# Key stacks of 128 rows with zeros, returned in two halves; key norms applied on GpSimd

## The chip, the cores and the metric

One core of one Trainium2 chip. The metric is the device time of one launch in microseconds. Its engines are named as in the profile: PE (TensorE, matmuls), PEld (its weight loads), DVE (VectorE), ACT (ScalarE), POOL (GpSimd), SP (SyncE, which issues all DMAs here; SPq is its queue).

## The reference

```python
# x: (32, 256, 256), context: (32, 77, 256); 8 heads of 128 in the cross-attention, 16 heads of 16 in the second
f_q, f_k, f_v = (proj(q), proj(k), proj(v))            # layer_norm(t) @ w_in.T, split into heads
dots = jnp.einsum('hqnd,hqmd->hqnm', f_q, f_k)
cosine_sim = dots / (qn[..., :, None] * kn[..., None, :])
var_component = jnp.einsum('hqn,hqm->hqnm', q_ratio, k_ratio)
cov_component = cosine_sim * decorr_scale
mixed = cw * cosine_sim + vw * cov_component + ww * var_component
out = jnp.einsum('hqnm,hqmd->hqnd', mixed, f_v)        # then @ w_out.T + b_out
...
x = x + jnp.tanh(g_xattn[0]) * out
...
scores = jnp.einsum('bqd,bkd->bkq', q, k) / 16         # 16 heads of 16, on layernorm(x)
attn = jax.nn.softmax(scores, axis=-1)
z = l2(l2(attended @ Wo) @ Wff); z = gelu(z)
x = x + jnp.tanh(g_ffn[0]) * z
```

`q_ratio`, `k_ratio` come from the variance of a row of `f_q`, `f_k`; `cw`, `vw`, `ww` and `decorr_scale` are eight numbers each, one per head. `f_k` and `f_v` are the same here, since the context serves as both.

## The kernel before

A setup phase (`setup_phase`, some 170 us) splits the weights into pairs of float16 halves `h` and `l`, normalizes the context, and leaves in DRAM `kstat`, whose rows 0 to 7 are one over the norm of each key and rows 8 to 15 its ratio. Then `main_phase` works on 16 pairs of batches, 512 rows of x each. Every engine walks through the same list of steps, `ORDER`, once in a turn; the work of three pairs overlaps in a turn, since `lead` gives each step the pair that it works on (0: the newest, 1: the one before, 2: the one before that). There are 18 turns; the first two and the last two leave steps out. An engine does its instructions strictly in this order, so a step that waits holds up what stands behind it on that engine.

The steps, by name. `fk`: projection of the context rows (PE), stored as `fvp` in halves (`.h` by ACT, `.l` by DVE; this is so for all products that are split). `fk.k`, `kh`, `kl`: the same values times one over the key's norm, `khat` (DVE, L1350), and its halves `kT` (ACT L1195, POOL L1288). `z`, `zT`: normalized rows of x and their transposes. `q`: projection of x, read by DVE for its statistics only (L1362). `G`: `kT` times the weights. `d`: `xT` times `G`, the dots, which DVE scales by `sq` into `mixed` (L1386). `x`: POOL makes `tmp` = key ratio times query ratio (L1296) and adds it to `mixed` (L1301). `V`: `fvp` times `w_out`. `m`: transposes of `mixed`. `y`: their product with `V`, added by DVE to `xb`, which is x plus a bias from POOL (L1277), into `x2S` (L1395). `ln1`, `lpow`, `ln2`, `zz`: the next normalization. `pq`, `pk`, `pv`: projections for the second attention. `S`: a score step, two matmuls (L1154). `M`: the row maximum (DVE, L1428). `X`: exp with its sum (ACT, L1237). `R`: `vsp` = v over the sums (DVE, L1442). `P`: attended values (PE, L1166). `E`, `L`: their halves. `O`: output product, and `F`: norms, gelu and the sum for `out`.

The 16 heads have only 16 channels each. To bring the parts q and k (their halves `h` and `l`) into the right rows, SP stores them to DRAM (step `parts`, L1033: four stores), and loads them back in another arrangement (step `back`, L1042): for c in 0 to 3 and e in 0 to 1, 16 rows of `kstack` and 16 rows of `qstack` with 512 columns for each of 8 heads. A score product contracts over the 64 rows of one half e:

```python
                        last = nc.tensor.matmul(sc[n % SC][:, jj * NQ:(jj + 1) * NQ],
                                                stack["k"][64 * e:64 * e + 64, j, b2 * NQ + k * P:b2 * NQ + (k + 1) * P],
                                                stack["q"][64 * e:64 * e + 64, j, b2 * NQ:(b2 + 1) * NQ],
                                                start=True, stop=True)
```

Scores 0 to 15 of a turn belong to the first batch of the pair (b2 = 0), 16 to 31 to the second. The first one waits until all 16 loads have landed. `krows` holds a piece of `kstat` for the pair, broadcast to all partitions; SP loads it twice in a turn, the norms (`ldk`, L1023) and the ratios (`ldr`, L1027).

Of the kernel before, what the change touches and what calls it, by code (L numbers as in the profile page):

```python
# [813 lines left out]
S17 E0 y0 x3 R3 X16 V5.h V5.l M17 X17 ldk m3 y0.o S18 m3.h m4 M18 m5 P3 m4.h L0 m3.l m5.h X18 S19 m4.l S20 m5.l fk0
M19 M20 S21 z fk0.h y1 E1 X19 L1 X20 fk0.l M21 fk0.k R4 zT0 O0 y1.o zT0.h ln1 X21 S22 fk1 zT0.f O0. M22 S23 lpow O1
fk1.h M23 X22 fk1.l S24 ln2 X23 P4 O1. fk1.k zz0 zT0.l S25 zz0.h zz1 fk2 zz0.l zz1.h kh0 zT1 zz1.l fk2.h S26 kl0 zT1.h
pq0 fk2.l fk2.k zT1.f M24 pq1 pq0.h M25 X24 pq0.l pk0 R5 X25 M26 pq1.h zT1.l S27 pk0.h pk1 pq1.l X26 pk0.l S28 M27
pk1.h P5 X27 pk1.l M28 S29 parts S30 M29 X28 q0 M30 X29 R6 S31 X30 q1 M31 q0.o X31 P6 kh1 R7 back E2 kl1 P7 L2 pv0 E3
# [676 lines left out]
```

## Time and profile before

| | us |
|---|---|
| median of three runs | 1545.8 (1540.1 to 1548.1) |
| the profiled execution | 1551.8 |
| its span, first to last instruction | 1550.1 |
| PE busy | 1377.8 (89%) |
| DVE busy | 1224.7 (79%) |
| ACT busy | 1027.7 (66%) |
| POOL busy | 443.8 (29%) |
| chain that ended last | PE 30%, DVE 26%, issue 13%, ACT 7%, DMA 6% |

Busy time counts an instruction from its start to its end, and these overlap on an engine, by up to 0.2 us for PE, whose ends are modelled. What an instruction costs in a row of others is the distance from its start to the next one's start, its pitch. The chain is the work followed back from the last instruction.

### The profile page before, as it was taken

To read this page: it belongs to the slowest core of one execution; us is meant where nothing else is said; L and a number is where in the kernel's file an instruction comes from. 1 tells how busy PE (TensorE), PEld (TensorE's weight loads), DVE (VectorE), ACT (ScalarE), POOL (GpSimd) and SP (SyncE) were. 2 spreads that over 40 slices of the span, in tenths; PEclk is the share of its full clock that TensorE was granted. 3 is DMA by queue.
4 is the path that set the end of the run, shared out by engine and by line. 5 is a ranking of instruction groups with operands and counts; after the bars stand their busy time and mean duration, and the time that the engine had idled before them with its cause. 6 is when DMAs were issued, how large, how long until landed. Compare 5 with 4: busy or idle time off the path is not lost.

```text
span 1550.1 us, 35088 instructions
## 1 busy us (share of the span) xinstructions
PE 1377.8 (89%) x10624; PEld 817.0 (53%) x10624; DVE 1224.7 (79%) x3180; ACT 1027.7 (66%) x3326; POOL 443.8 (29%) x279
## 2 busy tenths in 40 slices
PE   5888488799999999999999999999999999999855
PEld 2655355455555555555565645555555555555422
DVE  5878656687979888888798888887888889797844
ACT  5564213575767676767677676777776768676766
POOL 1441241314141323233232424141414141414100
PEclk9999599899999999999999999999999999999966
DMA  8420103417070707070716243343535261717060
GB/s 255 142 87 17 31 22 70 72 49 107 16 138 16 138 16 138 16 133 21 111 43 93 61 74 80 60 78 67 86 61 94 51 103 43 111 25 117 15 95 15
DMA packets 125733, 115.12 MB, mean 74 GB/s; under 512 B 8024, under 2 KB 123376, under 8 KB 125680
## 3 DMA queue, kind: packets, MB, share of 16 engines
q1 hardware_dynamic: 125696, 114.66, 38.4%
q8 instruction: 19, 0.31, 0.1%
q14 instruction: 18, 0.15, 0.0%
HBM read 78.40 MB, written 25.32 MB: 67 GB/s over the span
## 4 chain that ended last, share of the span: by engine, by line
PE 30%; DVE 26%; issue 13%; ACT 7%; DMA 6%; SPq 3%; DVEq 1%; POOL 0%; PEldq 0%; ACTq 0%; POOLq 0%; PEld 0%
PE work L749 8%; PE work L751 7%; PE work L750 7%; DVE nm L1428 7%; DMA qstack<-parts 5%; ACT prob L1237 5%; PE score L1154 3%; SPq L1042 3%; PE attended L1166 2%; PE work L1073 2%; DVE vsp L1442 2%; DVE mixed L1386 2%; DVE zz L1408 1%; DVE l2s L1401 1%; DMA parts<-kl 1%
## 5 line engine op out<-in xcount | busy, mean ns | idle before, releaser
L1237 ACT ACTIVATE prob<-score,nm 128x256 f32<-128x256 f32 x1024 | 474.5, 480 | 117.2 <-DVE nm L1428 112.6
L1428 DVE TENSOR_REDUCE nm<-score 128x2 f32<-128x512 f32 x512 | 336.1, 682 | 32.0 <-PE score L1154 31.2
L1154 PE MATMUL score<-qstack,kstack 64*128 64x256 f16 x1024 | 184.2, 281 | 42.1 <-DMA qstack<-parts 22.9
L1237 ACT ACTIVATION_READ_ACCUMULATOR prob<-score,nm 128x1 f32 x1024 | 216.4, 211 | 0.0
L1362 DVE BATCH_NORM_STATS2 qst<-work 128x6 f32<-128x128 f32 x512 | 111.1, 284 | 72.0 <-PE work L751 70.8
L1166 PE MATMUL attended<-prob,vsp 128*32 128x256 f32 x2048 | 143.4, 399 | 22.4 <-DVE vsp L1442 22.4
L1154 PEld LDWEIGHTS score<-qstack,kstack 64*128 64x128 f16 x1024 | 59.2, 96 | 175.3 <-ACT prob L1237 90.7
L1301 POOL TENSOR_TENSOR mixed<-mixed,tmp 128x616 f32<-128x616 f32 x64 | 96.0, 1501 | 177.4 <-DVE mixed L1386 173.7
L1281 POOL TENSOR_TENSOR rq<-qft,mhalf 128x32 f32<-128x32 f32 x16 | 87.0, 5439 | 144.8 <-DVEq L1369 144.8
L1288 POOL TENSOR_TENSOR kTl<-khat,kTh 128x462 f16<-128x462 f32 (+1 forms) x48 | 46.3, 966 | 253.8 <-ACT kTh L1195 253.8
L749 PE MATMUL work<-woutTh,fvph 128*128 128x256 f16 x384 | 107.3, 279 | 0.0
L750 PE MATMUL work<-woutTl,fvph 128*128 128x256 f16 x384 | 106.6, 278 | 0.0
L751 PE MATMUL work<-woutTh,fvpl 128*128 128x256 f16 x384 | 106.5, 277 | 0.0
L749 PE MATMUL work<-wTh,xTh 128*128 128x512 f16 x256 | 98.3, 384 | 4.3 <-DVE xTl L1356 2.4
L1166 PEld LDWEIGHTS attended<-prob,vsp 128*32 128x32 f32 x2048 | 54.9, 112 | 83.0 <-issue 47.0
L1216 ACT ACTIVATE Gh<-work 128x462 f16<-128x462 f32 (+1 forms) x96 | 47.5, 512 | 76.8 <-PE work L751 75.9
L750 PE MATMUL work<-wTl,xTh 128*128 128x512 f16 x256 | 97.8, 382 | 0.0
L751 PE MATMUL work<-wTh,xTl 128*128 128x512 f16 x256 | 97.8, 382 | 0.0
L1442 DVE TENSOR_TENSOR vsp<-v,rs 128x128 f32<-128x128 f32 x128 | 79.7, 622 | 16.9 <-DVE rs L1436 4.3
L749 PE MATMUL work<-Vph,mTh 128*128 128x256 f16 (+1 forms) x320 | 89.3, 279 | 0.0
L750 PE MATMUL work<-Vpl,mTh 128*128 128x256 f16 (+1 forms) x320 | 88.6, 277 | 0.0
L751 PE MATMUL work<-Vph,mTl 128*128 128x256 f16 (+1 forms) x320 | 88.6, 277 | 0.0
(291 smaller groups left out, 3573.7 us busy)
## 6 DMA issues: line engine op xcount, KB each, us to landing
krows<-kstat SPq DMA_DIRECT2D x32, 616.0 KB, 5.8
kstack<-parts SPq DMA_DIRECT2D x128, 128.0 KB, 7.8
qstack<-parts SPq DMA_DIRECT2D x128, 128.0 KB, 8.3
s_xin<-in_x SPq DMA_DIRECT2D x8, 1024.0 KB, 6.0
xin<-in_x SPq DMA_DIRECT2D x16, 512.0 KB, 7.4
x<-x2S SPq DMA_DIRECT2D x16, 512.0 KB, 5.3
out<-zb SPq DMA_DIRECT2D x16, 512.0 KB, 4.9
parts<-qh SPq DMA_DIRECT2D x16, 256.0 KB, 2.2
```

The lines of the kernel that those rows point to most:

```text
L749: nc.tensor.matmul(out, a["h"][at], b["h"][bt], start=first, stop=False)
L750: nc.tensor.matmul(out, a["h"][at], b["l"][bt], start=False, stop=False)
L751: return nc.tensor.matmul(out, a["l"][at], b["h"][bt], start=False, stop=last)
L1154: last = nc.tensor.matmul(sc[n % SC][:, jj * NQ:(jj + 1) * NQ], stack["k"][64 * e:64 * e + 64, j, b2 * NQ + k * P:b2 * NQ + (k + 1) * P], ...
L1166: last = nc.tensor.matmul(pvb[t][32 * j:32 * j + 32, 0:NQ], vsp[:, e, k, j, :], prob[:, n % PG, k, j, :], start=(e == 0 and k == 0), stop= ...
L1216: nc.scalar.activation(dst, src, ACT.Copy, scale=scale).then_inc(hi_ready[lead(e)], 1)
L1237: nc.scalar.activation(prob[:, g % PG, k, u % 4, :], sc[n % SC][:, jj * NQ:(jj + 1) * NQ], ACT.Exp, bias=nm[:, u:u + 1], accum_out=sums[:, ...
L1281: nc.gpsimd.tensor_tensor(rq[:], qft[:, 0, :, :], w["mhalf"][:].rearrange("p (t h) -> p t h", h=H), ALU.pow).then_inc(rq_ready, 1)
L1301: nc.gpsimd.tensor_tensor(mixed[:, t % 2, :], mixed[:, t % 2, :], tmp[:], ALU.add).then_inc(mixed_ready, 1)
L1362: last = nc.vector.bn_stats(qst[:, t, 4 * half + h, :], bank(e)[:, h * DH:(h + 1) * DH])
L1428: nc.vector.tensor_reduce(nm[:, 2 * n:2 * n + 2], sc[n % SC][:, :].rearrange("p (u q) -> p u q", q=NQ), AX.X, ALU.max, negate=True).then_i ...
L1442: nc.vector.tensor_tensor(vsp[:, e, :, :, FD * e:FD * (e + 1)], src, bc(rs[:, units].rearrange("p (k j) -> p k j", k=KT).unsqueeze(3), [P, ...
```

## The change

It does five things. The key stack gets a second plane: for e = 0 its rows 64 to 127 are zeros, for e = 1 its rows 0 to 63; POOL writes the zeros once, and a score product contracts over all 128 rows of `qstack`. The return of the stacks is cut into `back0` and `back1`, one for each batch, with 16 loads of half the columns each, and the scores wait for their own half. `khat`, `kT` and their steps are gone: G works on `fvp`, and POOL multiplies the scaled dots by one over the key's norm, a third instruction in each x step; both parts of `krows` are loaded at once. `xb` is gone: x is loaded a second time (`ldy`), into `x2S`, where POOL adds the bias. And `ORDER` is another list.

```diff
-xb G0 G0.h G1 G2 G1.h G0.l G2.h G1.l G3 ldr G2.l G4 qs1 G3.h ldx V0 G4.h S0 V0.h G3.l S1 qpow S2 G4.l G5 M0 V1 G5.h
...
+qs1 S0 G0 S1 G0.h G1 S2 G1.h G2 G0.l qpow G2.h G1.l G3 G2.l G4 ldr M0 G3.h V0 M1 G4.h X0 G3.l G4.l G5 V0.h M2 S3 V1
...
-    krows = sb("krows", [P, H, PM])
-    fvp, kT, G, Vp = pair("fvp", [P, PADW]), pair("kT", [P, H, PM]), pair("G", [P, KT, H * PM]), pair("Vp", [P, 2, HT, DIM])
+    krows = sb("krows", [P, 2, H, PM])
+    fvp, G, Vp = pair("fvp", [P, PADW]), pair("G", [P, KT, H * PM]), pair("Vp", [P, 2, HT, DIM])
...
-    stack = {a: sb(a + "stack", [P, FH // 2, PR], F16) for a in "qk"}
+    qstack, kstack = sb("qstack", [P, FH // 2, PR], F16), sb("kstack", [P, 2, FH // 2, PR], F16)
...
+                elif step == "ldy":
+
+                    sp_wait(zz_ready, a)
+                    sp_wait(x2_in, a * 16)
+                    sp.dma_start(x2S[:], x_rows[bass.ds(a * PR, PR), :].rearrange("(t p) d -> p t d", p=P)).then_inc(y_in, 16)
                 elif step == "ldr":
 
                     sp_wait(mixed_ready, a * PT)
+                    sp.dma_start(krows[:], kstat[:, bass.ds(a * PM, PM)].rearrange("(s h) n -> s h n", h=H)
+                                 .partition_broadcast(P)).then_inc(kr_in, 16)
...
-                elif step == "back":
-
-                    sp_wait(parts_stored, a * 64 + 64)
-                    sp_wait(sc_ready, a * SCORES + START)
+                elif step in ("back0", "back1"):
+
+                    b2 = int(step[-1])
+                    cols = slice(b2 * NQ, (b2 + 1) * NQ)
+                    if b2 == 0:
+                        sp_wait(parts_stored, a * 64 + 64)
+                    sp_wait(sc_ready, a * SCORES - (1 - b2) * SCORES // 2 + SC_CREDIT)
                     for c in range(4):
                         for e in range(2):
...
+                            rows = slice(64 * e + FD * c, 64 * e + FD * (c + 1))
+                            for dst, n in ((kstack[rows, e, :, cols], 2 + c // 2), (qstack[rows, :, cols], c % 2)):
+                                src = parts[n].rearrange("(q e d) n -> e d q n", e=2, d=FD)[e][:, :, cols]
+                                sp.dma_start(dst, src).then_inc(stack_in[b2], 16)
...
-                                        w["wN"], (ALL, h, slice(k * P, (k + 1) * P)), kT, (ALL, h))
+                        keys = {half: key_cols(half, h, h + 1) for half in "hl"}
+                        last = products(nc, bk[:, (h - lo_h) * PM:(h - lo_h + 1) * PM].rearrange("p (b m) -> p b m", m=MK),
+                                        w["wN"], (ALL, h, slice(k * P, (k + 1) * P)), keys, (ALL,))
...
-                    if n == 0:
-                        pe.wait_ge(stack_in, b * 256 + 256 + START)
+                    if n % (SCORES // 2) == 0:
+                        pe.wait_ge(stack_in[b2], b * 256 + 256 + START)
...
-                                                stack["k"][64 * e:64 * e + 64, j, b2 * NQ + k * P:b2 * NQ + (k + 1) * P],
-                                                stack["q"][64 * e:64 * e + 64, j, b2 * NQ:(b2 + 1) * NQ],
+                                                kstack[:, e, j, b2 * NQ + k * P:b2 * NQ + (k + 1) * P],
+                                                qstack[:, j, b2 * NQ:(b2 + 1) * NQ],
...
+            nc.gpsimd.memset(kstack[:], 0.0).then_inc(init, 1)
...
                 if e == "xb":
 
-                    pool.wait_ge(x_ready, a * 16 + 16)
-                    pool.wait_ge(v2_ready, a)
-                    nc.gpsimd.tensor_tensor(xb[:], xin[:], bc(w["tb"][:].unsqueeze(1), [P, PT, DIM]),
+                    pool.wait_ge(y_in, a * 16 + 16)
+                    nc.gpsimd.tensor_tensor(x2S[:], x2S[:], bc(w["tb"][:].unsqueeze(1), [P, PT, DIM]),
                                             ALU.add).then_inc(xb_ready, 1)
...
                     pool.wait_ge(tmp_ready, a * PT + t + 1)
                     wait_drained(pool, a, f"d{2 * t}", f"d{2 * t + 1}")
+                    rows = mixed[:, t % 2, :].rearrange("p (h m) -> p h m", m=MK)
+                    nc.gpsimd.tensor_tensor(rows, rows, krows[:, 0, :, (t // 2) * MK:(t // 2 + 1) * MK],
+                                            ALU.mult).then_inc(dotted, 1)
+                    pool.wait_ge(dotted, a * PT + t + 1)
                     nc.gpsimd.tensor_tensor(mixed[:, t % 2, :], mixed[:, t % 2, :], tmp[:], ALU.add).then_inc(mixed_ready, 1)
...
-                elif part == "k":
-
-                    lo_h, hi_h = HEAD_PARTS[int(c)]
-                    dve.wait_ge(rk_in, a * 16 + 16)
-                    ins = nc.vector.scalar_tensor_tensor(
-                        khat[:, lo_h:hi_h, :], bank(e)[:, 0:(hi_h - lo_h) * PM].rearrange("p (h n) -> p h n", n=PM), KS,
-                        krows[:, lo_h:hi_h, :], ALU.mult, ALU.mult)
                     drain(ins, e)
```

What the order moves, at the three places of which the prediction speaks. First SP's queue from the last store of `parts` to the store of the result, in the loop over turns; `kstack` and `qstack` are the loads of `back`. Before:

```order
L1033 DMA parts<-kl 128x2x512
L1005 ISA
L1005 ISA [waits parts_stored]
L1042 DMA kstack<-parts 16x8x512 [waits sc_ready]
L1042 DMA qstack<-parts 16x8x512
...
L1053 ISA [waits ob_ready]
L1053 DMA out<-zb 128x4x256
```

With the change:

```order
L1035 DMA parts<-kl 128x2x512
L1005 ISA
L1005 ISA [waits parts_stored]
L1048 DMA kstack<-parts 16x8x256 [waits sc_ready]
L1048 DMA qstack<-parts 16x8x256
...
L1005 REGISTER_ALU
L1048 DMA kstack<-parts 16x8x256 [waits sc_ready]
L1048 DMA qstack<-parts 16x8x256
...
L1058 ISA [waits ob_ready]
L1058 DMA out<-zb 128x4x256
```

The loads are of 256 columns instead of 512, and a second row of eight pairs stands behind the first, ahead of the store of the result; only its first load waits, for the scores of the turn.

Second, PE at the turn of the loop, up to the first score (`wTh,xTl` is the end of q7, `wNh` is G, `woutTh` the end of V0). Before:

```order
L751 MATMUL work<-wTh,xTl 128x512
L988 UNCONDITIONAL_BRANCH
L988 ISA
L1090 ISA [waits drained0]
L749 MATMUL work<-kTh,wNh 128x154 [waits kT_ready]
L750 MATMUL work<-kTl,wNh 128x154
...
L751 MATMUL work<-woutTh,fvpl 128x256
L1149 ISA
L1151 ISA [waits stack_in]
L1154 MATMUL score<-qstack,kstack 128x256 [waits exp_done]
L1154 MATMUL score<-qstack,kstack 128x256
```

With the change (`wvh,zzTl` is the end of pv1):

```order
L751 MATMUL work<-wvh,zzTl 128x256
L987 UNCONDITIONAL_BRANCH
L987 ISA
L1158 ISA [waits stack_first]
L1161 MATMUL score<-qstack,kstack 128x256 [waits exp_done]
L1161 MATMUL score<-qstack,kstack 128x256
L937 ISA
L934 ISA [waits drained0]
L749 MATMUL work<-fvph,wNh 128x154 [waits drained0]
L750 MATMUL work<-fvpl,wNh 128x154
```

The first score stands ahead of G0, right behind pv1; before, G0 to G4 and V0 stood ahead of it, and pv1 in the middle of the q steps.

Third, POOL's x steps, x0 and the beginning of x1. Before:

```order
L1295 REGISTER_ALU [waits wqr_ready,kr_in]
L1296 TENSOR_TENSOR tmp<-krows,wqr 128x616 [waits mixed_ready]
L1299 REGISTER_ALU
L934 ISA [waits tmp_ready]
L1301 TENSOR_TENSOR mixed<-mixed,tmp 128x616 [waits drained1,drained0]
L1296 TENSOR_TENSOR tmp<-krows,wqr 128x616 [waits mixed_ready,wqr_ready,kr_in]
```

With the change:

```order
L1290 REGISTER_ALU [waits wqr_ready,kr_in]
L1291 TENSOR_TENSOR tmp<-krows,wqr 128x616 [waits mixed_ready]
L1294 REGISTER_ALU
L934 ISA [waits tmp_ready]
L934 ISA [waits drained2]
L1297 TENSOR_TENSOR mixed<-mixed,krows 128x616 [waits drained0]
L1300 TENSOR_TENSOR mixed<-mixed,tmp 128x616 [waits dotted]
L1291 TENSOR_TENSOR tmp<-krows,wqr 128x616 [waits mixed_ready,wqr_ready,kr_in]
```

A multiplication by `krows`, the key norms, stands between the two that were there, and behind the wait for the dots.

## Rows read from the trace of the kernel before

**Rows 1.** Windows: one turn; us, busy of PE, PEld, DVE, ACT, POOL, PEclk, DMA share, GB/s

```profile
748.73:829.47 80.74, 75.92 (x626) 44.79 (x625) 69.02 (x169) 58.40 (x196) 24.13 (x15) 1.00 0.43 74
```

**Rows 2.** Timeline, SP's queue: first store of parts, 13 turns apart; start, duration

```profile
425.67 0.37 SPq L1033 DMA_DIRECT2D parts<-qh  x1
...
1470.06 0.36 SPq L1033 DMA_DIRECT2D parts<-qh  x1
```

**Rows 3.** Waits of PE in that turn, first and last of seven (4.5 us)

```profile
PE attended L1166 <- DVE vsp L1442: 1.4, 2, 1.1
...
PE work L749 <- DVE qst L1362: 0.2, 1, 0.2
```

**Rows 4.** Waits of DVE in that turn, first and last of ten (9.6 us)

```profile
DVE qst L1362 <- PE work L751: 4.0, 2, 3.6
...
DVE qft L786 <- DVE qft L770: 0.2, 1, 0.2
```

**Rows 5.** Timeline, SP's queue, one turn

```profile
747.99 0.37 SPq L1033 DMA_DIRECT2D parts<-qh  x1
...
752.67 0.33 SPq L1042 DMA_DIRECT2D kstack<-parts  x1
...
759.67 0.43 SPq L1042 DMA_DIRECT2D qstack<-parts  x1
...
771.43 0.41 SPq L1027 DMA_DIRECT2D krows<-kstat  x1
...
828.73 0.37 SPq L1033 DMA_DIRECT2D parts<-qh  x1
```

**Rows 6.** Timeline, PE: the turn's first score products

```profile
773.42 0.82 PE L1154 MATMUL score<-qstack,kstack 64*128 64x256 f16 x6 [0.81 <-DMA qstack<-parts]
```

**Rows 7.** Timeline, PE: a score pair between projections, one before a P step

```profile
824.60 0.38 PE L750 MATMUL work<-zzTl,wkh 128*128 128x512 f16 x1
824.81 0.38 PE L751 MATMUL work<-zzTh,wkl 128*128 128x512 f16 x1
825.12 0.39 PE L1154 MATMUL score<-qstack,kstack 64*128 64x256 f16 x2
825.45 0.39 PE L749 MATMUL work<-zzTh,wkh 128*128 128x512 f16 x1
...
826.85 0.39 PE L1154 MATMUL score<-qstack,kstack 64*128 64x256 f16 x2
827.17 1.07 PE L1166 MATMUL attended<-prob,vsp 128*32 128x256 f32 x16
```

**Rows 8.** Windows (columns as Rows 1): the stacks' return; a load of key rows

```profile
756.00:770.00 14.00, 13.23 (x88) 7.26 (x86) 10.22 (x34) 8.53 (x20) 4.67 (x3) 1.00 1.17 111
...
802.00:806.00 4.00, 4.00 (x44) 2.55 (x42) 3.20 (x6) 3.09 (x10) 0.00 (x0) 1.00 0.80 154
```

**Rows 9.** Groups by line and form: busy, mean ns; idle before

```profile
L1442 DVE TENSOR_TENSOR vsp<-v,rs 128x128 f32<-128x128 f32 x128 | 79.7, 622 | 16.9 <-DVE rs L1436 4.3
L1350 DVE SCALAR_TENSOR_TENSOR khat<-work,krows 128x462 f32<-128x462 f32 x32 | 20.2, 631 | 0.3 <-DMA krows<-kstat 0.3
L1301 POOL TENSOR_TENSOR mixed<-mixed,tmp 128x616 f32<-128x616 f32 x64 | 96.0, 1501 | 177.4 <-DVE mixed L1386 173.7 <-POOL tmp L1296 3.4
```

**Rows 10.** Timeline, POOL and DVE: the extra step and what it holds up

```profile
778.52 1.23 POOL L1296 TENSOR_TENSOR tmp<-krows,wqr 128x616 f32<-128x616 f32 x1 [1.03 <-DMA krows<-kstat]
786.33 1.22 POOL L1296 TENSOR_TENSOR tmp<-krows,wqr 128x616 f32<-128x616 f32 x1 [0.17 <-POOL mixed L1301]
...
786.58 1.12 DVE L1442 TENSOR_TENSOR vsp<-v,rs 128x128 f32<-128x128 f32 x1
```

**Rows 11.** One line's instructions, L1442: ns min/median/max

```profile
L1442 DVE TENSOR_TENSOR vsp<-v,rs x128: 291/293/1470, 296.3 to 1531.8; 128x128 f32<-128x128 f32 x128
```

**Rows 12.** Timeline, PE: first turn with m0; first scores of the last turn

```profile
224.04 1.07 PE L1117 MATMUL work<-ident,mixed 128*128 128x128 f32 x8 [0.83 <-POOL mixed L1301]
...
1494.02 1.46 PE L1154 MATMUL score<-qstack,kstack 64*128 64x256 f16 x6 [8.78 <-DMA qstack<-parts]
```

More of the change, by code:

```diff
@@ L814 @@
[L814 to L818, printed above, removed]
@@ L819 @@
-kh2 L3 q1.o O2 pv0.v O3 O2. q2 O3. q3 F1 q2.o pv1 q3.o kl2 F2 q4 pv1.v q5 q4.o F3 q6 q5.o q7 q6.o q7.o F4 out res
+qs1 S0 G0 S1 G0.h G1 S2 G1.h G2 G0.l qpow G2.h G1.l G3 G2.l G4 ldr M0 G3.h V0 M1 G4.h X0 G3.l G4.l G5 V0.h M2 S3 V1
+G5.h V0.l X1 G5.l X2 qs2 S4 M3 d0 V1.h M4 S5 X3 V1.l d1 ldy ldx d0.o X4 d2 d1.o M5 S6 S7 M6 d3 X5 x0 R0 V2 X6 M7 S8 P0
+d2.o X7 M8 d3.o S9 V2.h S10 X8 M9 V3 M10 X9 R1 x1 S11 V3.h V4 M11 X10 V2.l S12 V4.h P1 M12 X11 V3.l S13 X12 V4.l xb m0
+M13 m1 m0.h R2 S14 d4 m1.h m0.l X13 S15 m1.l m2 m2.h d4.o d5 E0 M14 S16 d5.o P2 X14 m2.l x2 M15 d6 M16 X15 S17 L0 V5
@@ L820 @@
+q5 q3.o F3 q4.o q6 back1 q5.o q7 q6.o pv0 q7.o F4 pv1 pv0.v pv1.v out res
 """.split()
@@ L829, in lead @@
         return 2
-    return 0 if step.split(".")[0].rstrip("0123456789") in ("z", "zT", "fk", "kh", "kl", "q", "ldx", "ldk") else 1
+    return 0 if step.split(".")[0].rstrip("0123456789") in ("z", "zT", "fk", "q", "ldx") else 1
 HALVES = [[s[:-2] for s in ORDER if s.endswith(".h") and s[:2] != "zT" and lead(s) == n] for n in range(2)]
@@ L952, in emptied @@
             lo_h, hi_h = HEAD_PARTS[c]
-            rows = fvp[half][:, 0:2 * H * PAD].rearrange("p (n c) -> p n c", c=PAD)
-            return (rows[:, 2 * lo_h:2 * hi_h, 127:PAD],
+            return (key_cols(half, lo_h, hi_h),
                     bk[:, 0:(hi_h - lo_h) * PM].rearrange("p (n m) -> p n m", m=MK), FV / WS)
@@ L996, in _ @@
         def _(sp):
-            for waited in (stack_in, ob_ready, vs_ready, sc_ready, stored):
+            for waited in (*stack_in, ob_ready, vs_ready, stored):
                 sp.sem_inc(waited, START)
+            sp.sem_inc(sc_ready, SC_CREDIT)
             sp.sem_inc(exp_done, EXP_CREDIT)
@@ L1038, in a_part @@
                     for c in range(4):
                         for e in range(2):
-                            for name, n in (("k", 2 + c // 2), ("q", c % 2)):
-                                src = parts[n].rearrange("(q e d) n -> e d q n", e=2, d=FD)[e]
-                                sp.dma_start(stack[name][64 * e + FD * c:64 * e + FD * (c + 1), :, :],
-                                             src).then_inc(stack_in, 16)
+                            rows = slice(64 * e + FD * c, 64 * e + FD * (c + 1))
@@ L1190, in a_part @@
                 e, _, part = e.partition(".")
-                if e in ("kh0", "kh1", "kh2"):
-                    lo_h, hi_h = HEAD_PARTS[int(e[-1])]
-                    wait_drained(act, a, "fk" + e[-1])
-                    nc.scalar.activation(kT["h"][:, lo_h:hi_h, :], khat[:, lo_h:hi_h, :], ACT.Copy).then_inc(kT_half, 1)
-                elif e[:-1] == "zT" and part in ("h", "f"):
+                if e[:-1] == "zT" and part in ("h", "f"):
                     c, bk = int(e[-1]), bank(e)
```

64 lines of the change are left out of this document (26 added, 38 removed).

## The prediction

> **What bounds the kernel now.** I read the windows of one turn first, then the waits of PE and of DVE, then SP's queue. The program is a setup, two turns without scores, and 16 turns with 32 score steps each. I call T0 the moment at which SP issues the first store of `parts`; it comes once in a turn, 16 times in all, so 15 full intervals lie between them. The reader is to see that an interval takes 80.7 us in the middle [rows 5], 80.3 us on average over 13 of them [rows 2], and that in one of them PE is busy 75.9 us and DVE 69.0, at the full clock, 2.4 GHz [rows 1]. PE waits for others 4.5 us in it [rows 3], so it is occupied for 80.7 - 4.5 = 76.2 us. DVE waits 9.6 us [rows 4], so it is occupied for 71.1. **PE's queue is the bound and DVE stands close behind it**; ACT (58.4 busy) and POOL (24.1) are not. DVE's longest wait, 4.0 us, is for the projections of q, the stage in which PE has work and DVE little.
>
> That stage exists because of a round trip. After T0 the four stores take until the first load of the stacks is issued at T0 + 4.7, the last of 16 loads is issued at T0 + 11.7 [rows 5], and PE's first score of the turn runs at 773.42, T0 + 25.4, after waiting 0.8 us for the last load [rows 6]. Until then PE fills the time with q, O, pv, G and V.
>
> **The change, part by part.**
>
> *128-row scores.* A matmul of 512 columns starts 0.21 to 0.22 us after the one before. From the last projection to the score pair it is 0.31, and from the pair, which needs 2 x 0.11, to the next projection 0.33 [rows 7]. A score step between ordinary products thus costs about 0.42 us where its columns ask for 0.22: 0.10 is lost on going in and 0.10 on coming out. The likeliest reason is that the array is regrouped, since these are the only products on 64 rows. In the timeline of that turn I count 17 runs of score steps with ordinary products on both sides and 8 next to a P step, which is itself in another shape, so that only one side is saved there. This gives 17 x 0.2 + 8 x 0.1 = **4.2 us a turn** off PE. The bounds are 0 (the gap stays) and 32 x 0.2 = 6.4. The Trainium skill, "TensorEngine Tiling (Array Packing)", section Theoretical Speedup, speaks against the padding: a contraction of 64 rows may run as two tiles side by side, up to 2 times as fast. In the trace the pair is not side by side (0.22 plus the two losses), since both of its products use the same half of the rows; by the rule a kernel that paired the halves would stand 32 x 0.11 = 3.5 us a turn better than this one, which neither of the two kernels does.
>
> *Return in two halves.* The loads are bound by bytes at 111 GB/s while they run [rows 8]. 2 MB at that rate is 18.9 us; the observed T0 + 4.7 to T0 + 25.3 is 1.7 more. The first half has 16 loads of 64 KB, 1 MB: 4.7 + 9.4 + 1.7 = T0 + 15.9. Below it is bounded by issue, 0.47 us from one load to the next [rows 5], 16 x 0.47 = 7.5 us, so T0 + 13.9. Above, if a packet costs the same at 512 bytes as at 1 KB, a half costs what the whole did: T0 + 25.3. I take the byte rate, as packets of 616 bytes move at 154 GB/s [rows 8], faster than is needed here. In the new order PE has after T0: P7 1.1 [rows 7]; q1 to q7, O2 and O3, six products of 512 columns each, 9 x 1.3 = 11.7; pv0 and pv1, 24 of 256 columns, 2.6; or 15.4 us. So **the wait for the stacks stays near 0.5 us**, and G, V0 and V1 run beside scores instead of ahead of them. The second half lands where the whole did, T0 + 25.3, half a turn before score 16.
>
> *Key norms.* khat (two of 0.63 and one shorter) goes from DVE, about 1.5 us a turn at its pitch [rows 9], and three activations from ACT and three subtractions from POOL, which nothing waits for long. POOL gets four multiplications of 616 columns, priced as the addition of that size, 1.50 us each [rows 9]: 6.0 us a turn. Each stands in the chain d, x, m. x0 starts with a product of 1.23 us when the key rows land, 778.52, T0 + 30.5 [rows 10]. One load of 1232 KB instead of 616 adds 616 KB at 154 GB/s, 4.0 us: T0 + 34.5. x0 and x1 then take 2 x (1.23 + 1.50 + 1.50) = 8.5, so m0 may start at T0 + 43. PE gets to m0 after 14 scores, at (76.6 - 16) / 32 = 1.9 us a score from T0 + 16: T0 + 42.6. The cost is 0.4 us; 0 to 3 is possible.
>
> *What POOL does to DVE.* vsp needs 0.29 us alone and 0.62 on average [rows 9, 11]; at 786.58 it takes 1.12 and ends with the product that POOL began at 786.33 [rows 10]. That is 8 x 0.33 = 2.6 us a turn for 10.9 us of x steps, 0.24 us per us. The new multiplications add 6.0 x 0.24 = **1.5 us on DVE**, 0 to 6.0. DVE's occupation stays at 71.1 - 1.5 + 1.5 = 71.1 us.
>
> *Rest.* The second load of x (512 KB) and the third use of x2S as xb lie in queues that are empty then: 0. POOL's memset of the key stack stands before the first turn, where POOL has nothing to do until qpow: 0 to 1 us, once.
>
> *Sum of a turn.* PE 76.2 - 4.2 = 72.0 occupied; its waits 4.5, less 0.3 for the stacks and plus 0.4 for m0: **76.6 us, 4.1 less**. DVE's 71.1 leaves 5.5 for its waits, of which the q stage keeps 4.0: it just fits. Bounds: 73.5 if most waits go, 79.2 if DVE keeps 8 us of its 9.6.
>
> *The ends.* In the first turn with x steps nothing else covers them, and PE waited 0.8 us for m0 already [rows 12]; four multiplications are 6.0, some of it behind V: +4. After the last T0 (1470.06 [rows 2]) the first score ran at 1494.02 [rows 12], 24.0 later, with nothing to fill the time; now 15.9, so -8.0, and about -1.3 for scores at the low clock.
>
> *Total.* 15 x -4.1 = -61.5, +4, -9.3: -66.8. The profiled execution took 1551.8 us for a span of 1550.1; it becomes 1485.0. It lies 6.0 above the median of the three runs, 1545.8, so I forecast **1479 us**.
>
> **The rivals.**
>
> *A. The halves are bound by packets, not bytes (slower).* Then the first half lands at T0 + 25.3, PE has 15.4 us of work before it and stands idle 9.4 more: a turn of 86, 15 x 5.3 + 4 = +83, **1629 us**. It decides from a loss of 4.1 us a turn on, that is when one 64 KB load takes over (15.4 + 4.1 - 4.7 - 1.7) / 16 = 0.82 us instead of 0.59. For it: the new pieces are smaller than any that this path has shown. Against: 616-byte pieces at 154 GB/s.
>
> *B. DVE becomes the bound.* Scores crowd it, POOL holds its vsp and DVE keeps 8 us of waits: 79.2 a turn, 15 x -1.5 + 4 - 9.3, **1518 us**. The Trainium skill, "SBUF — State Buffer", section Who interferes with whom, says that a vector instruction with two SBUF inputs and a GpSimd one that reads SBUF exclude each other for a whole instruction, and the trace agrees (vsp, 1.12 against 0.29). If each of the four multiplications held DVE for its whole 1.50 us where PE waits, a turn would be 4.5 longer than in my sum, 81.1, and the total about **1546 us**, no change.
>
> *C. The padding saves nothing.* If the gap of 0.10 comes with semaphores and not with the shape, a turn stays at 80.8 and only the end gains: **1541 us**. Against: V, y and q steps also begin with a wait for a semaphore and follow at their pitch.
>
> *D. The waits melt with the gaps*, as they are DVE's lateness in the score stage, which now starts 9.5 us earlier: 73.5 a turn, **1432 us**.
>
> **How the numbers follow.** Forecast 0.57, A 0.09, B as 1518 0.16 and as no change 0.03, C 0.07, D 0.08. A measurement here tells 0.5%, about 8 us, from no change. Faster: 0.57 + 0.16 + 0.08 = 0.81. C and the second form of B come to 0.10, of which 0.02 could land above the edge: same 0.08, slower 0.09 + 0.02 = 0.11. The range takes in D nearly and B: 1436 to 1518.
>
> **What would show it.** The profile of the changed kernel should show an interval between first stores of `parts` of 76 to 77 us; from the last projection to a score pair 0.22 us and from the pair on 0.22; the first score of a turn 16 us after T0; additions and multiplications of 1.5 us on POOL, and vsp at a mean of 0.65 to 0.85 us. I am wrong if the interval is above 79 us, if DVE's waits stay at 9 us, or if the first score stands later than T0 + 18.

## The result, and the profile after

The changed kernel takes **1594.5 us** (median of four runs, 1592.4 to 1596.5), the kernel before 1546.7 us on the same chip: a ratio of 1.031, 95% interval 1.029 to 1.034. It is slower by 3.1%; the forecast was 1479 us. The page of its profiled execution (share of the span by engine; the granted clock in 40 slices; the chain that ended last):

```profile
span 1594.7 us, 35158 instructions
...
PE 1344.9 (84%) x10624; PEld 882.7 (55%) x10624; DVE 1181.2 (74%) x3132; ACT 997.1 (63%) x3278; POOL 493.3 (31%) x296
...
PEclk9999699998999999899999899989999999999977
...
PE 21%; SPq 15%; ACT 13%; DMA 13%; issue 10%; POOL 9%; DVE 7%; POOLq 0%; DVEq 0%; ACTq 0%; PEldq 0%; PEld 0%
```

PE is busy less than before, in a longer span. The chain no longer runs mostly over PE and DVE but over SP's queue, the DMAs, ACT and POOL; in its list by line, the loads of the stacks on SP's queue hold 12% and the load of `krows` 10%. The sum over the program: the first T0 moved from 257.7 to 267.4 (+9.7), the 15 intervals from 80.8 to 83.6 us on average (+41.6), and the piece from the last T0 to the end from 80.0 to 73.3 (-6.7). That is the 44.6 us between the two spans.

One of the shorter turns, T0 at 772.17, with a stretch of it, in windows (columns as in Rows 1), which answers to [rows 1]:

```profile
772.17:854.51 82.34, 73.59 (x626) 48.82 (x625) 65.01 (x166) 56.58 (x191) 26.84 (x16) 0.98 0.42 79
812.17:816.17 4.00, 2.20 (x11) 2.02 (x12) 0.42 (x1) 0.79 (x2) 3.92 (x3) 0.64 0.00 0
```

Its waits of PE, the two longest of six (8.8 us in all, 4.5 before [rows 3]):

```profile
PE work L1124 <- POOL mixed L1300: 5.7, 1, 5.7
PE work L1124 <- DVE x2S L1383: 1.0, 1, 1.0
```

SP's queue in that turn, which answers to [rows 5] (`krows` is issued behind all 32 loads of the stacks):

```profile
772.17 0.37 SPq L1035 DMA_DIRECT2D parts<-qh  x1
...
776.85 0.32 SPq L1048 DMA_DIRECT2D kstack<-parts  x1
...
791.44 0.43 SPq L1048 DMA_DIRECT2D qstack<-parts  x1
792.35 0.41 SPq L1058 DMA_DIRECT2D out<-zb  x1
793.15 0.50 SPq L1053 DMA_DIRECT2D x<-x2S  x1
794.38 0.41 SPq L1027 DMA_DIRECT2D krows<-kstat  x1
...
854.51 0.37 SPq L1035 DMA_DIRECT2D parts<-qh  x1
```

POOL's x0 and x1 in the same turn, timeline:

```profile
805.01 1.22 POOL L1291 TENSOR_TENSOR tmp<-krows,wqr 128x616 f32<-128x616 f32 x1 [10.43 <-DMA krows<-kstat]
806.48 1.38 POOL L1297 TENSOR_TENSOR mixed<-mixed,krows 128x616 f32<-128x616 f32 x1 [0.25 <-POOL tmp L1291]
807.94 1.49 POOL L1300 TENSOR_TENSOR mixed<-mixed,tmp 128x616 f32<-128x616 f32 x1
809.60 1.22 POOL L1291 TENSOR_TENSOR tmp<-krows,wqr 128x616 f32<-128x616 f32 x1 [0.17 <-POOL mixed L1300]
810.98 1.38 POOL L1297 TENSOR_TENSOR mixed<-mixed,krows 128x616 f32<-128x616 f32 x1 [0.16 <-POOL tmp L1291]
812.44 1.48 POOL L1300 TENSOR_TENSOR mixed<-mixed,tmp 128x616 f32<-128x616 f32 x1
```

And PE around m0, timeline, with the first score of the turn ahead of it:

```profile
788.49 0.39 PE L1161 MATMUL score<-qstack,kstack 128*128 128x256 f16 x2 [0.42 <-DMA qstack<-parts]
...
807.86 0.39 PE L1161 MATMUL score<-qstack,kstack 128*128 128x256 f16 x2
813.97 1.97 PE L1124 MATMUL work<-ident,mixed 128*128 128x128 f32 x8 [5.72 <-POOL mixed L1300]
815.73 0.63 PE L1161 MATMUL score<-qstack,kstack 128*128 128x256 f16 x2
```

Read these three together. `krows` is issued at T0 + 22.2, behind 32 loads of stacks and two stores, and lands 11.0 us later (median; 5.8 for half the size before). POOL begins x0 at T0 + 32.8 and ends x1 at T0 + 41.8. PE had come to m0 at T0 + 36.1 and stood there for 5.7 us. Around the end of that idle stretch the granted clock was 0.64 on average over 4 us, a mixture of 1.2 and 2.4 GHz. It fell while PE still stood, the eight transposes of m0 took 1.97 us, and it was back at 2.4 GHz by 816.8. About 2.8 us of work at half speed are 1.4 us lost. The wait and the low clock make 7.1 us; without them this turn would be 75.2.

Most turns lose more than this one. PE comes to m0 at T0 + 36.1 in 13 of the 15 intervals, waits for it 94.1 us in 16 waits over the whole run, and the granted clock is 0.92 to 0.98 in the 15 intervals, against 1.00 in 11 of 15 before. The longest one, in windows:

```profile
433.88:519.98 86.10, 76.44 (x626) 50.98 (x625) 64.71 (x166) 56.80 (x191) 26.76 (x16) 0.92 0.41 76
```

The score products did gain what they were meant to. Around a pair in PE's timeline:

```profile
820.48 0.29 PE L751 MATMUL work<-Gh,xTl 128*128 128x308 f16 x1
820.62 0.38 PE L1161 MATMUL score<-qstack,kstack 128*128 128x256 f16 x2
820.83 0.27 PE L749 MATMUL work<-woutTh,fvph 128*128 128x256 f16 x1
```

The pair starts 0.14 after the product of 308 columns before it, which is that product's own pitch, and the next product starts 0.21 after the pair, which is the pair's 2 x 0.11. The two losses of 0.10 [rows 7] are gone. The first score runs at T0 + 16.3.

### The profile page after: what moved, and what is told of

It is laid out like the page before. It is cut to its first block, busy times and chain, and to the rows that moved or that the text cites. A ratio compares the mean times of both kernels' runs of the same rounds, so it can differ in the third digit from the quotient of the medians.

```text
span 1594.7 us, 35158 instructions
## 1 busy us (share of the span) xinstructions
PE 1344.9 (84%) x10624; PEld 882.7 (55%) x10624; DVE 1181.2 (74%) x3132; ACT 997.1 (63%) x3278; POOL 493.3 (31%) x296
## 4 chain that ended last, share of the span: by engine, by line
PE 21%; SPq 15%; ACT 13%; DMA 13%; issue 10%; POOL 9%; DVE 7%; POOLq 0%; DVEq 0%; ACTq 0%; PEldq 0%; PEld 0%
SPq L1048 12%; DMA krows<-kstat 10%; ACT prob L1239 8%; PE work L749 5%; PE work L750 5%; PE work L751 5%; POOL mixed L1300 3%; POOL mixed L1297 3%; DMA parts<-kl 3%; POOL tmp L1291 2%; DVE z L1332 2%; PE work L1124 2%; PE score L1161 2%; PE attended L1173 1%; ACT junk L1256 1%
## 5 line engine op out<-in xcount | busy, mean ns | idle before, releaser
L1416 DVE TENSOR_REDUCE nm<-score 128x2 f32<-128x512 f32 x512 | 341.0, 684 | 41.3 <-PE score L1161 38.9
L1239 ACT ACTIVATION_READ_ACCUMULATOR prob<-score,nm 128x1 f32 x1024 | 228.5, 223 | 0.0
L1161 PE MATMUL score<-qstack,kstack 128*128 128x256 f16 x1024 | 194.7, 285 | 30.4 <-DMA qstack<-parts 18.0
L1124 PE MATMUL work<-ident,mixed 128*128 128x128 f32 (+1 forms) x320 | 63.0, 345 | 115.9 <-POOL mixed L1300 94.1
L1161 PEld LDWEIGHTS score<-qstack,kstack 128*128 128x128 f16 x1024 | 89.3, 101 | 100.6 <-ACT prob L1239 36.0
L1308 POOL TENSOR_TENSOR nrs<-nrm,phalf 128x8 f32<-128x8 f32 x16 | 26.2, 1636 | 354.5 <-ACT zb L1258 354.5
L1291 POOL TENSOR_TENSOR tmp<-krows,wqr 128x616 f32<-128x616 f32 x64 | 78.8, 1231 | 174.2 <-DMA krows<-kstat 168.8
L1218 ACT ACTIVATE mTh<-work 128x512 f16<-128x512 f32 (+1 forms) x96 | 47.1, 534 | 126.8 <-PE work L1124 126.7
L1340 DVE SCALAR_TENSOR_TENSOR mTl<-work,mTh 128x512 f16<-128x512 f32 (+1 forms) x96 | 54.7, 598 | 94.9 <-ACT mTh L1218 94.8
L1124 PEld LDWEIGHTS work<-ident,mixed 128*128 128x128 f32 (+1 forms) x320 | 46.7, 175 | 128.6 <-POOL mixed L1300 90.5
L1297 POOL TENSOR_TENSOR mixed<-mixed,krows 128x616 f32<-128x616 f32 x64 | 89.4, 1396 | 58.7 <-DVE mixed L1375 49.3
```

The lines of the kernel that those rows point to most:

```text
L1124: last = nc.tensor.transpose(bk[0:HM_ROWS[t], (2 * n + r) * P:(2 * n + r + 1) * P], mixed[:, r, t * P:t * P + HM_ROWS[t]], ident[:])
L1239: nc.scalar.activation(prob[:, g % PG, k, u % 4, :], sc[n % SC][:, jj * NQ:(jj + 1) * NQ], ACT.Exp, bias=nm[:, u:u + 1], accum_out=sums[:, ...
L1291: nc.gpsimd.tensor_tensor(tmp[:].rearrange("p (h m) -> p h m", m=MK), krows[:, 1, :, (t // 2) * MK:(t // 2 + 1) * MK], bc(wqr[:, t, :].uns ...
L1297: nc.gpsimd.tensor_tensor(rows, rows, krows[:, 0, :, (t // 2) * MK:(t // 2 + 1) * MK], ALU.mult).then_inc(dotted, 1)
L1416: nc.vector.tensor_reduce(nm[:, 2 * n:2 * n + 2], sc[n % SC][:, :].rearrange("p (u q) -> p u q", q=NQ), AX.X, ALU.max, negate=True).then_i ...
```

## The experiments

All times are medians; ratios are to the kernel before on the same chip. An edit is to the changed kernel unless it says otherwise. Theory 1: the key rows come late because of where their load stands in SP's queue, and PE stands at m0 for them. Theory 2: the multiplications on GpSimd cost the time, wherever the rows are. Experiments 1 to 4, 5 to 8 and 9 to 12 are three sessions, in which the kernel before took 1542.1, 1543.0 and 1547.3 us (1546.7 beside the changed kernel), so a difference of medians across sessions is good to about 5 us.

**1. The key rows loaded early.**

```diff
-... G2.l G4 ldr M0 ...
+... G2.l G4 M0 ...
-... M18 x3 z S20 ...
+... M18 x3 ldr z S20 ...
-("z", "zT", "fk", "q", "ldx")
+("z", "zT", "fk", "q", "ldx", "ldr")
```

> The changed kernel, with the load of the key rows (ldr) moved on SP's queue from behind the two returns of the stacks to right behind x3 of the turn before, some 27 us ahead of T0; it loads for the next pair there. Theory 1 (late key rows): in the changed kernel krows is issued at T0 + 22.2 and its x steps begin at T0 + 32.8, so x1 ends at T0 + 41.8 while PE stands at m0 from T0 + 36.1; that costs 5.9 us of wait and about 1.5 us of half clock behind it in each turn. With the rows there early, x0 can start at T0 + 24 (query norms) and x1 ends by T0 + 35, so the wait for m0 falls below 1 us, the granted clock stays at 1.00 there, a turn takes 76 to 77.5 us instead of 83.6, and the total is 1485 to 1505 us. Theory 2 (the four multiplications on GpSimd are the cost, through the longer chain and DVE's locks, whenever the rows land): the gain is at most 1 us a turn, total 1580 or more.

Measured: 1507.3 us, 0.977 (0.974 to 0.979), 87 us less than the changed kernel and less than the kernel before; 2 us above the range of Theory 1. POOL, timeline of a turn with T0 = 654.22:

```profile
676.60 1.22 POOL L1291 TENSOR_TENSOR tmp<-krows,wqr 128x616 f32<-128x616 f32 x1
681.28 1.39 POOL L1297 TENSOR_TENSOR mixed<-mixed,krows 128x616 f32<-128x616 f32 x1 [3.46 <-DVE mixed L1375]
...
687.89 1.52 POOL L1300 TENSOR_TENSOR mixed<-mixed,tmp 128x616 f32<-128x616 f32 x1
```

x1 now ends at T0 + 35.2. In two neighbouring turns, windows:

```profile
577.10:654.22 77.12, 72.52 (x626) 47.82 (x625) 65.26 (x165) 56.58 (x191) 26.81 (x16) 1.00 0.46 84
654.22:732.99 78.77, 74.16 (x626) 48.90 (x625) 65.25 (x165) 56.53 (x191) 26.82 (x16) 0.98 0.46 83
```

There is no wait for m0 in either. They differ by 1.65 us of low clock only, which Theory 1 had not expected here. Seven of the 15 intervals have such a stretch, at about T0 + 55. Theory 1 explains the larger part of the loss, 87 of the 115 us between the forecast and the changed kernel; Theory 2 as it was stated is out.

**2. No multiplication by the norms** (this part of the computation is left out), rows still late.

```diff
-                    nc.gpsimd.tensor_tensor(rows, rows, krows[:, 0, :, (t // 2) * MK:(t // 2 + 1) * MK],
-                                            ALU.mult).then_inc(dotted, 1)
-                    pool.wait_ge(dotted, a * PT + t + 1)
```

> The changed kernel without the multiplication by one over the key's norm on GpSimd (this part of the computation is left out); krows is loaded as before, late. Theory 1: x0 and x1 end 2 x 1.46 us earlier, so of the 5.9 us that PE waits for m0 3 remain, and part of the low clock; a turn takes 79.5 to 80.5, total 1530 to 1550 us. Theory 2: all of the loss goes with the multiplications, the wait for m0 falls below 1 us and the total to 1500 or less.

Measured: 1511.5 us, 0.980 (0.978 to 0.983). In PE's waits of one turn (T0 = 730.09) the one for m0 is what was expected:

```profile
PE work L1124 <- POOL mixed L1296: 3.1, 1, 3.1
```

3.1 us instead of 5.7, a turn of 78.5. But the total is 83 us lower, not 50: some 8.6 us in the first turn (its T0 is 258.8, not 267.4), and in each turn something besides m0. Neither theory had that, and the total lies 18 us below the range of Theory 1. DVE's timeline has one thing that changed (experiment 6 says more): a group of four `z` instructions takes 1.38 us in this run and 3.69 in the changed kernel.

**3. Scores on 64 rows.** `kstack[64 * e:64 * e + 64, e, ...]` and `qstack[64 * e:64 * e + 64, ...]` in the product, nothing else.

> The changed kernel with score products on 64 rows of the same stacks (the padding unused). Theory 1: the 13 scores ahead of m0 lie in time that PE would wait anyway, so only the other 19 cost: 19/32 of 4.2 us, 2.5 us a turn, total about 1630 us; the gaps around a score pair are back at 0.10 on each side. If PE's occupation set the whole turn, it would be 4.2 us a turn, 1658 us. If the padding had saved nothing (rival C of the prediction), 1594 us.

Measured: 1631.0 us, 1.055 (1.050 to 1.060). The padding is worth 36 us even here, and Theory 1's number holds. The trace agrees with its reason: PE comes to m0 later, at T0 + 37.3 to 37.8 in 13 of 15 intervals, and waits for it less, by 24.7 us over these intervals, so what the scores ahead of m0 cost is mostly taken from the wait. The comparison is not quite clean: with 64 rows the four `z` instructions take 2.62 us instead of 3.69, as they meet only one of POOL's instructions.

**4. The kernel before, scores over 128 rows.** `stack["k"][:, j, ...]` and `stack["q"][:, j, ...]`, nothing else; each score then sums both halves of the channels.

> The kernel before with score products over all 128 rows of both stacks (no zero planes: the sums mix the two halves of the channels, so the scores are others; shape and work of every other instruction are the same). It measures the padding in the old order by itself. By the prediction's sum: 4.2 us a turn off PE, 15 x 4.2 plus 1.3 at the end, total about 1482 us, if DVE lets it through; if DVE is the bound close behind (rival B) about 1.5 us a turn, 1525 us; if nothing is saved 1546 us. I expect 1490 to 1505, since DVE kept 9.6 us of waits.

Measured: 1532.1 us, 0.993 (0.990 to 0.996), a gain of 10 us, far from the 1490 to 1505 expected and 7 us short of the 1525 of rival B. One turn in windows, and PE's two longest waits in it:

```profile
736.59:815.82 79.23, 73.08 (x625) 47.82 (x626) 67.50 (x169) 58.71 (x194) 24.12 (x15) 1.00 0.43 75
```

```profile
PE attended L1166 <- DVE vsp L1442: 1.7, 2, 1.1
PE score L1154 <- ACT prob L1237: 1.7, 5, 0.4
```

PE's waits in the turn sum to 6.2 us, so it is occupied for 73.0 us, 3.2 less than before the change of shape; the turn is only 1.5 shorter than [rows 1], because PE's waits grew from 4.5 to 6.2 us, over the whole run those for ACT's `prob` from 14.1 to 25.7. The chain that ended last now goes over DVE for 30% of the span and over PE for 26% (26% and 30% before). In the old order the score stage, DVE's maxima and ACT's exp with it, takes back half of what PE saves.

**5. The early rows with scores on 64 rows** (edits 1 and 3 together).

> The kernel with the early key rows (1507 us) and score products on 64 rows of the same stacks. With no wait for m0 left, PE's occupation sets the turn, so the padding should be worth its full 4.2 us a turn here: 77.9 + 4.2 = 82.1, total 1507 + 15 x 4.2 + 1.3, about 1570 us, slower than the kernel before. If DVE shares the bound (rival B) it is worth half of that or less: 1540 or below.

Measured: 1554.6 us, 1.007 (1.005 to 1.010), between the two expectations. The padding is worth 47 us in this order, against 10 in the old one and 36 with the late rows; here too `z` is held less with 64 rows (2.62 us instead of 3.80), so 47 is rather too little. How much the padding gives depends on the order. What the new order gives by itself was not tried: no run has it with the key norms where they were.

**6. The early rows without the multiplications** (edits 1 and 2; that part of the computation is left out).

> The kernel with the early key rows and no multiplication by the key norms on GpSimd (left out of the computation). It measures what the multiplications cost when the rows are there in time. Prediction's terms: 4 us in the first turn and up to 1.5 us a turn through DVE's locks where DVE counts. If PE alone sets the turn: only the first turn's 5 to 8 us, total about 1500 us. If the locks count: 15 x 1.5 more, 1478 us.

Measured: 1450.6 us, 0.941 (0.939 to 0.943): 57 us for the multiplications where the rows are not late, 3.3 us a turn and 6 in the first (of the 3.3, about 0.8 is the low clock of seven turns, which has gone too). That is beyond the upper of the two expectations, 29 us. Where it goes stands in DVE's timeline of experiment 1; the first line is the first of four `z` instructions, the second the group of four:

```profile
700.73 1.59 DVE L1332 TENSOR_SCALAR z<-xin,st 128x256 f32<-128x256 f32 x1
```

```profile
700.73 3.80 DVE L1332 TENSOR_SCALAR z<-xin,st 128x256 f32<-128x256 f32 x4
```

and POOL at the same time:

```profile
700.78 1.39 POOL L1297 TENSOR_TENSOR mixed<-mixed,krows 128x616 f32<-128x616 f32 x1 [0.23 <-POOL tmp L1291]
702.25 1.49 POOL L1300 TENSOR_TENSOR mixed<-mixed,tmp 128x616 f32<-128x616 f32 x1
```

The first z ends just behind POOL's multiplication and the second just behind its addition; only then do the last two follow at their own pace. POOL's two instructions are no longer than elsewhere, though the first z is recorded 0.05 us ahead of the multiplication. Four z take 3.80 us. In the kernel before, with POOL idle, DVE's timeline has:

```profile
807.80 1.38 DVE L1333 TENSOR_SCALAR z<-xin,st 128x256 f32<-128x256 f32 x4
```

The changed kernel has the same picture, z first, POOL second (here the first z slips through and the second and third are held):

```profile
824.03 3.69 DVE L1332 TENSOR_SCALAR z<-xin,st 128x256 f32<-128x256 f32 x4
```

```profile
824.20 1.48 POOL L1297 TENSOR_TENSOR mixed<-mixed,krows 128x616 f32<-128x616 f32 x1 [0.23 <-POOL tmp L1291]
825.76 1.49 POOL L1300 TENSOR_TENSOR mixed<-mixed,tmp 128x616 f32<-128x616 f32 x1
```

The Trainium skill, "SBUF — State Buffer", section Who interferes with whom, names `tensor_scalar` among the DVE operations that can take both ports and then exclude GpSimd for a whole instruction. The trace agrees: 1.59 us for one z beside a multiplication of 1.39, against 0.41 alone (the mean in the kernel before). The longest case stands in the first turn: POOL's memset of the zeros, 7.06 us, held one z for 7.09 us. Little came of it: the first T0 of experiment 2, which has this memset, is 1.1 us later than in the kernel before.

```profile
177.03 7.06 POOL L1273 MEMSET kstack<- 128x8192 f16 x1
```

```profile
176.66 8.22 DVE L1332 TENSOR_SCALAR z<-xin,st 128x256 f32<-128x256 f32 x4
```

**7. The kernel before, return in two halves, nothing else.**

> The kernel before with the return in two halves and nothing else, in its own order. In it G0 to G4 and V0 stand ahead of the first score, which waits only 0.8 us for the stacks, so a turn can gain at most 0.8 us; the last turn, where nothing fills the time, gains up to 8 us. Expected 1527 to 1540 us. If the halves were bound by packets (rival A), there would be no gain at the end, and 1546 us or more.

Measured: 1533.8 us, 0.993 (0.991 to 0.996), as expected. Thirteen of the 15 intervals stay at 79.9 to 80.8 us; the gain is in the ends. The stretch behind the last T0 is 73.4 us instead of 80.0. Between the profiled executions the first two intervals are shorter too (77.9 and 80.6 against 83.0 and 84.9), with less low clock in them. The first scores of its last turn (T0 = 1458.69), PE's timeline:

```profile
1475.78 0.92 PE L1161 MATMUL score<-qstack,kstack 64*128 64x256 f16 x6 [3.38 <-DMA qstack<-parts]
```

T0 + 17.1 instead of 24.0. So the half does not take the time of the whole, as it would if packets bound it.

**8. The early rows, and z elsewhere.** z goes to a place where POOL is idle (edit 1 and this one):

```diff
-... M18 x3 ldr z S20 ...
+... M18 x3 ldr S20 ...
-... m5.l M22 S24 ...
+... m5.l M22 z S24 ...
```

> The kernel with the early key rows and one step moved in the order: z (four DVE instructions of 0.95 us in a row, 3.8 us) from behind x3 to behind M22. In the 1507 us kernel PE waits behind that block for Vpl (0.4) and x2S (1.0), ACT waits 3.6 us for a maximum, and in about half of the turns PE's clock falls to half for 3.4 us right after (78.8 against 77.1 us a turn). Theory (the block starves PE, and the low clock follows from it): the waits and the low spells go, a turn takes 75.5 to 76.5 us, total 1475 to 1490 us. Rival (PE's occupation is the bound and the low clock has another cause): no change or within 5 us of 1507.

Measured: **1464.9 us, 0.951 (0.948 to 0.953)**, the fastest of the kernels that leave nothing out, 42 us below experiment 1 and 10 below the range of the theory. z in DVE's timeline, and one turn in windows:

```profile
694.96 1.38 DVE L1332 TENSOR_SCALAR z<-xin,st 128x256 f32<-128x256 f32 x4
```

```profile
641.20:716.12 74.92, 72.02 (x626) 47.91 (x625) 62.68 (x165) 56.50 (x191) 27.20 (x16) 1.00 0.48 87
```

z takes 1.38 us again, no low clock is left in that turn, and 14 of 15 intervals are 74.9 to 76.1 us. PE waits 3.0 us, so it is occupied for 71.9.

**9. The same without the multiplications** (left out of the computation).

> The 1465 us kernel (early key rows, z behind M22) without the multiplications by the key norms (left out of the computation). With z beside x3 they cost 57 us (1507 to 1451). Theory: most of that was one collision, the four z instructions taking 3.8 us beside POOL's multiplication and addition of x3 instead of 1.4, and the starved stretch behind them; now z stands where POOL is idle, so leaving them out gives only the first turn's 5 to 6 us and the one vsp that is held (0.9 us a turn): total 1444 to 1456 us. Rival: the multiplications cost 3.4 us a turn wherever z stands: total 1410 us.

Measured: 1440.3 us, 0.931 (0.928 to 0.934). 24.6 us are left of the 57 (20.9 between the spans of the profiled executions: 4.2 in the first turn and 1.1 in each interval). So the larger part, 32 us by the medians and 36 by the spans, went with the collision with z, the low clock behind it included. The rest is a little more than expected: 1440 us is 4 below the range.

**10. z elsewhere with the rows still late.**

> The changed kernel with z moved behind M22 and nothing else: krows is still loaded late. If the two costs are separate (wait for m0; z held by POOL), it gains what z gave with the early rows, 42 us: 1550 us. If the late rows are the one bound of the loop, since ldr waits for x3, nothing is gained, 1590 us. I expect 1545 to 1565: PE's path from m0 to the next T0 gets shorter and the path from T0 to m0 stays.

Measured: 1566.9 us, 1.014 (1.010 to 1.017), 28 us less than the changed kernel, between "separate" (42) and "nothing" and 2 above the range. The wait for m0 in one turn:

```profile
PE work L1124 <- POOL mixed L1300: 6.5, 1, 6.5
```

The wait is what it was, 97.3 us over the run against 94.1, so nothing is given back in front of m0. Where the other 14 us are shows in the intervals. Moving z gave 2.2 us a turn in the turns of experiment 1 that have no low clock (77.1 to 74.9), and gives 2.0 here on average (83.6 to 81.6). With the early rows it also took away the low clock of seven turns, 1.65 us each. Here the low clock comes with the wait for m0 and stays, a granted clock of 0.94 to 0.98 in every interval. The two costs are nearly separate.

**11. The second half of the stacks behind the key rows**: `back1` stands behind `ldr`, in the next turn of the loop, and `ldr` keeps its place in its turn.

```diff
-... q6 back1 q5.o ...
+... q6 q5.o ...
-... G2.l G4 ldr M0 ...
+... G2.l G4 ldr back1 M0 ...
```

> The changed kernel with the second half of the return (back1) moved on SP's queue behind the store of the result and the load of krows, in the next turn of the loop; ldr keeps its place in its turn. krows is then issued 7.7 us earlier, at about T0 + 14.5, and starts behind 1 MB of stacks instead of 2. Theory 1 (place in SP's queue and what is ahead of it in the transfers): x1 ends by T0 + 36, the wait for m0 is 0 to 1 us, total 1500 to 1515 us, as with the early load; the second half lands near T0 + 32, well ahead of score 16. If it is the size of the load (1232 KB at once) that matters, the rows stay late: over 1560 us.

Measured: 1506.4 us, 0.973 (0.970 to 0.977), the same as experiment 1 and within Theory 1's range. SP's queue in one turn:

```profile
738.09 0.37 SPq L1035 DMA_DIRECT2D parts<-qh  x1
...
755.63 0.41 SPq L1027 DMA_DIRECT2D krows<-kstat  x1
```

The load is issued at T0 + 17.5, behind one half only, POOL begins x0 at T0 + 27.9 and PE waits 0.5 us for m0. It is as large as before, so the size alone does not make it late; moving it up in the queue is enough. (The size is in the time to landing all the same: 616 KB took 5.8 us before, 1232 KB 7.8 with the stacks long landed.) (It is issued 4.7 us earlier, not the 7.7 expected: SP waits 3.2 us for DVE's `zb`, which the store of the result ahead of it needs.)

**12. V3 ahead of P0** in the kernel of experiment 8 (`M7 S8 V3 P0`).

> The 1465 us kernel with V3 moved ahead of P0, so that PE has 1.6 us of work while POOL's addition of x0 holds vsp (1.54 us instead of 0.29), where it now waits 0.9 us. If the wait is simply covered: 15 x 0.9 off, 1452 us. If another wait takes its place (V3's bank, the scores behind): within 4 us of 1465.

Measured: 1499.8 us, 0.970 (0.966 to 0.973), 35 us slower than experiment 8 (39 between the spans of the profiled executions); both expectations missed. PE's longest wait in a turn:

```profile
PE work L749 <- DVE mixed L1375: 1.8, 1, 1.8
```

V3 needs a bank that DVE empties with a `mixed` step, and that step stands behind the very `vsp` that POOL holds. PE now waits for it ahead of P0 and of the score behind, and DVE then waits 2.2 us for that score. A second `vsp` is held as well, the one behind that score, 1.72 us instead of 0.29. PE comes to m0 at T0 + 38.9 instead of 37.1.

## Why the prediction was wrong

By its own steps, in its order:

- *128-row scores*: right in the mechanism. The losses on both sides of a pair are gone. PE's occupation fell by 3.2 us in the old order (experiment 4) and to 71.9 in the new (experiment 8), against 4.2 and 72.0 predicted. Whether it reaches the total depends on the order: 10, 36 or 47 us.
- *Return in two halves*: right. The first score stood at T0 + 16.3, predicted near 16, and the wait for the stacks was 0.4 us. Rival A is out, by this and by experiment 7.
- *Key norms*, **"PE gets to m0 after 14 scores, at 1.9 us a score from T0 + 16: T0 + 42.6. The cost is 0.4 us; 0 to 3 is possible."** This step failed. Its half about POOL was right: rows at T0 + 32.8 (34.5 predicted), x1 done at T0 + 41.8 (43). PE came to m0 at T0 + 36.1, 6.5 us earlier than I had it. I had spread the 32 scores evenly over the turn, but the projections stand in the other part of it; in the stretch up to m0 PE has 13 scores, not 14, and needs 19.8 us for all that stands there, 1.5 us a score. The order had shown what stands there. The cost, for which the sum had 0.4, was 5.7 us in the turn shown and 94.1 us in 16 waits over the run, and on top the low clock around the end of the wait, of which the prediction had nothing: 1.4 us in the turn shown, more in most others. Taking this away gave 87 us (experiment 1), with experiment 11 as the second way.
- *What POOL does to DVE*: **"The new multiplications add 6.0 x 0.24 = 1.5 us on DVE"**. This step failed too. The hold is real, but I priced it from `vsp`, by a mean over the turn, and let DVE's spare time take it, so that the turn paid nothing. In the new order `vsp` is held less (mean 367 ns, 622 before [rows 9]); what is held is `z`, which I did not look at: its mean went from 412 to 1077 ns (1008 without the four of the first turn). That is 2.3 us in one block, and PE and ACT wait behind it. With the early rows DVE is busy 65.25 us in a turn with the multiplications (experiment 1, T0 at 890.45) and 62.54 without (experiment 6, T0 at 856.97). These 2.7 lie within my 0 to 6.0; but the turn pays 3.3, where my sum had nothing. Moving z gave 42 us, or 28 with the late rows.
- *Rest*: the second load of x shows no cost in the turn read here, where POOL does not wait for it; no run tests it. The memset of the zeros cost about the 1 us that I had allowed, though it held DVE for 7 us.
- *The ends*: the first T0 came 9.7 us later, predicted 4; leaving out the multiplications alone takes 8.6 of it back, so the term was mis-sized and is almost wholly theirs. The tail gained 6.7, predicted 9.3: in the last turn the first load of the stacks is issued at T0 + 6.1 (4.6 in the kernel before) and the first scores ran at T0 + 18.1, not 15.9:

```profile
1539.48 1.46 PE L1161 MATMUL score<-qstack,kstack 128*128 128x256 f16 x6 [6.21 <-DMA qstack<-parts]
```

Rival B had a part in both failures of size: a faster PE meets DVE's and ACT's stage in the old order (experiment 4), and POOL holds DVE, but on another instruction than I had named. Rival C is out, and D's "waits melt" came true only in part: 3.0 us of waits in experiment 8, a turn of 74.9, between D's 73.5 and my 76.6. With the two failed steps repaired, by two moves in the order, the kernel takes 1465 us where I had said 1479. None of the rivals was the case that came: late key rows. I had the numbers for it, T0 + 43 against T0 + 42.6, and gave a meeting of two chains within 0.4 us a cost of 0 to 3, when an error of 6.5 in either arrival costs 6.5.

What stays open: why the granted clock falls in some turns of experiment 1 without a wait over 1 us in them (654.22 to 732.99) and not in others with nearly the same waits; in experiment 8 it falls in the first interval only. In the last turn SP waits 4.0 us for the last store of `parts`, 2.5 in the kernel before; why that store takes longer is open too. And what the 1.1 us a turn of experiment 9 consist of was not tried; `vsp`, at a mean of 438 ns with the multiplications and 294 without, 8 times a turn, would be 1.2 us, all of it, if each hold reached PE.

## What to carry to other kernels

- Where two chains meet, compute both arrivals from the work that stands in front of each, step by step, in the new order; the mean pace of a turn is no arrival time. Give the meeting the error of the arrivals as its range.
- On a queue that works in order, look at what is ahead of the load, not only at what it waits for: here two moves, the load a turn earlier or half of the stacks behind it, gave 87 and 88 us for the same bytes.
- Before more work goes to GpSimd, list what DVE does beside it in the new order, `tensor_scalar` included, and keep blocks of such instructions away from it.

## What the hardware showed that I had not expected

- A `tensor_scalar` of 128x256 with one tensor input in SBUF was held for a whole GpSimd instruction, 1.59 us instead of 0.41, and the next one for the following instruction again.
- The same happened beside a GpSimd memset, which reads no tensor: 7.06 us of memset, one `z` of 7.09 us.
- An idle stretch of 5.7 us on PE had a price behind it: the next 2.8 us ran at half clock, 1.97 us for eight transposes that took 1.09 elsewhere in that turn.
- A load of 1232 KB took 11.0 us to land behind 2 MB of stacks, 10.2 between the two halves, and 7.8 where it was issued long after the stacks (medians of experiments 11 and 1).
